# Attention with a second, transposed score product, and values and denominators of a group in one run of column-tiled products one step later

## The reference, cut to what matters

```
h = layernorm(x)
q = (h @ wq_w.T + wq_b).reshape(b, t, 32, 32)
k1 = h @ wk_w.T + wk_b            # one head of 32 for all
v1 = h @ wv_w.T + wv_b
scores = einsum('bqhd,bkd->bhqk', q, k1) / sqrt(32)
scores = where(causal, scores, -inf)
weights = softmax(scores)
attn = einsum('bhqk,bkd->bqhd', weights, v1)
x = x + attn.reshape(b, t, 1024) @ wo_w.T + wo_b
```

## Time and profile before

| | us |
|---|---|
| median of the runs | 3959.29 |
| profiled execution, span of the core | 3969.6 |
| TensorE matmul busy in it | 3404.7 |
| VectorE busy | 2089.3 |
| ScalarE busy | 1116.5 |
| GpSimd busy | 618.2 |

### The profile page before, as it was taken

The page is one execution under the profiler, slowest core; times in us unless marked ns, Lnnn a source line. Parts: engine busy times, 40 slices in busy tenths (PEclk is TensorE's granted clock), DMA queues, the critical chain, the costliest instruction groups (busy, mean ns, idle before and its releaser), DMA issues. The chain is left out here.

```text
span 3969.6 us, 53353 instructions
## 1 busy us (share of the span) xinstructions
PE 3404.7 (86%) x20224; PEld 2841.5 (72%) x20224; DVE 2089.3 (53%) x3582; ACT 1116.5 (28%) x2964; POOL 618.2 (16%) x754
## 2 busy tenths in 40 slices
PE   1898998998989989989999778878787878787868
PEld 1786887887868878878788356757575757666656
DVE  3463663654636626546466236555565646464633
ACT  2341442423414414324244013121212121121221
POOL 0001001000010010000100033223232323232311
PEclk9999999999999999999999778888898988888878
DMA  6322222222222222132221400000101010101000
GB/s 213 96 75 94 79 63 96 78 70 89 75 83 75 67 93 84 60 101 79 73 75 46 154 22 22 13 31 11 33 9 34 6 38 6 37 3 41 1 21 22
DMA packets 105455, 234.99 MB, mean 59 GB/s; under 512 B 20170, under 2 KB 38858, under 8 KB 105202
## 3 DMA queue, kind: packets, MB, share of 16 engines
q1 hardware_dynamic: 100544, 228.22, 18.6%
q10 hardware_dynamic: 4658, 3.22, 0.3%
HBM read 139.10 MB, written 41.94 MB: 46 GB/s over the span
## 5 line engine op out<-in xcount | busy, mean ns | idle before, releaser
L305 ACT ACTIVATE probs<-ps_attn,neg_max 128x128 f32<-128x128 f32 (+3 forms) x1024 | 534.8, 526 | 1070.5 <-DVE neg_max L398 1045.5
L557 PE MATMUL ps_attn<-probs_t,v_pad 128*128 128x128 f32 x5120 | 696.3, 277 | 17.5 <-DVE probs_t L408 15.9
L557 PEld LDWEIGHTS ps_attn<-probs_t,v_pad 128*128 128x128 f32 x5120 | 626.7, 192 | 33.6 <-DVE probs_t L408 28.2
L398 DVE TENSOR_REDUCE neg_max<-ps_attn 128x1 f32<-128x384 f32 (+3 forms) x704 | 449.8, 639 | 315.9 <-PE ps_attn L526 313.7
L408 DVE COPY probs_t<-ps_attn 128x512 f32<-128x512 f32 (+1 forms) x704 | 447.1, 636 | 272.4 <-PE ps_attn L544 272.4
L1182 PE MATMUL ps_mixer<-m_w_hi,m_xt_hi 128*128 128x512 f32 x1024 | 429.0, 419 | 77.1 <-DVE m_xt_lo L1021 77.1
L524 PE MATMUL ps_attn<-k_stack,q_stack 96*128 96x128 f32 (+3 forms) x1024 | 371.1, 398 | 72.9 <-issue 50.6
L1183 PE MATMUL ps_mixer<-m_w_hi,m_xt_lo 128*128 128x512 f32 x1024 | 415.6, 406 | 0.0
L1184 PE MATMUL ps_mixer<-m_w_lo,m_xt_hi 128*128 128x512 f32 x1024 | 414.2, 405 | 0.0
L544 PE MATMUL ps_attn<-ident_sb,probs 128*128 128x128 f32 x2560 | 397.5, 274 | 0.0
L544 PEld LDWEIGHTS ps_attn<-ident_sb,probs 128*128 128x128 f32 x2560 | 285.2, 142 | 20.3
(11 more groups left out here) (189 smaller groups left out, 5408.3 us busy)
## 6 DMA issues: line engine op xcount, KB each, us to landing
wq_hi<-wq_split SPq DMA_DIRECT2D x64, 512.0 KB, 3.6
wq_lo<-wq_split SPq DMA_DIRECT2D x64, 512.0 KB, 4.5
q_stack<-q_hi SPq DMA_DIRECT2D x512, 64.0 KB, 2.0
x_ring<-in_a_x SPq DMA_DIRECT2D x32, 512.0 KB, 4.1
q_stack<-q_lo SPq DMA_DIRECT2D x256, 64.0 KB, 2.0
r_ring<-in_a_x SPq DMA_DIRECT2D x32, 512.0 KB, 3.7
x<-r_ring SPq DMA_DIRECT2D x32, 512.0 KB, 2.6
m_xs<-x SPq DMA_DIRECT2D x32, 512.0 KB
```

The source lines that it names most:

```text
L305: exp = nc.scalar.activation(probs[:, s % P_RING, m * n:(m + 1) * n], ps[:, s % S_RING, m * n:(m + 1) * n], ACT.Exp, bias=neg_max[:, s % S ...
L398: nc.vector.tensor_reduce(neg_max[:, s % STAT, 0:len(heads)], ps[:, s % S_RING, 0:n * len(heads)].rearrange("p (j k) -> p j k", k=n), AX.X ...
L557: mm = nc.tensor.matmul(ps[:, 6 + g % 2, i * P:(i + 1) * P], v_pad[:, k, lead:lead + P], probs_t[:, u % T_RING, cols], start=(j == 0 and k ...
```

## The change

The attention function is rewritten; the mixer is not touched. What it does:

- Each score product is made twice. `scores` (queries on partitions) serve only for the row maxima (`tops`), for all 11 units of a group as before; the mask is now a float32r product, one per unit instead of one per head. The 16 maxima columns are transposed in one product (`tops_turned`), copied by ScalarE and written by one copy on SyncE's queue (`shift`) as a 97th row of `q_stack`, under which `k_stack` has a row of -1. `turned_scores` (keys on partitions, no mask, 11 units of at most 512 columns) then give score minus maximum already transposed.
- ScalarE takes the exponential of these straight into the tiles `pt` (no transposes, no copies); GpSimd sets what lies above the diagonal to zero (`cut`, four `affine_select` of 128x512 a group).
- One step later `weigh_all` multiplies values (`v_sb`, 128x32) and a tile of ones (128x32) with `pt` in float32: 4 key tiles x 2 x 4 heads = 32 products of 512 to 128 columns, each with 32 output partitions at 32*j. VectorE takes the reciprocal of the denominators (128x512) and multiplies (`divide`). This stands in place of the transposes, of the padded value products and of the `finish_` steps up to `finish_scale`; `finish_low` goes to GpSimd.
- There are no rows with barriers any more: steps M from -2 to 64 run through all 64 groups, written out, without a loop. Step M holds, in TensorE's order, the query projection of M+2, the maxima's transpose of M, scores 0 and 1 of M+1, the value products of M-1, then in turn the turned scores of M and the other scores of M+1. In a step with M+2 divisible by 8 the layer norm's transposes, the key and value projection and the whole query projection of the next row take the projection's place; a step with M divisible by 8 ends with the output projection of the row that is done.

The diff, cut to its core:

```diff
-    S_RING, P_RING, T_RING, STAT = 3, 3, 2, 8
-    T_LAG, AV_LAG = 2, 3
...
+    S_UNITS = [(3, (0,)), (3, (1,)), (3, (2,)), (3, (3,)), (2, (0,)), (2, (1,)), (2, (2,)), (2, (3,)), (1, (0, 1)), (1, (2, 3)),
+               (0, (0, 1, 2, 3))]
+    T_UNITS = [(0, (0,)), (0, (1,)), (0, (2,)), (0, (3,)), (1, (0,)), (1, (1,)), (1, (2,)), (1, (3,)), (2, (0, 1)), (2, (2, 3)),
+               (3, (0, 1, 2, 3))]
...
+                def stack(G):
+                    sp.wait_ge(qhi_done, G + 1)
+                    if G >= 2:
+                        sp.wait_ge(st_ready, U * (G - 1))
+                    for place, src in ((0, q_hi), (2, q_hi), (1, q_lo)):
+                        if place == 1:
+                            sp.wait_ge(qlo_done, G + 1)
...
+                def shift(G):
+                    sp.wait_ge(top_rows_done, G + 1)
+                    sp.dma_start(q_stack[KROWS:KROWS + 1, G % 2, :, :].bitcast(F32).rearrange("o j (i t) -> o (j i) t", t=P),
+                                 top_rows[:, :].bitcast(F32)).then_inc(top_in, DMA)
...
+                for M in STEPS:
+                    if inside(M):
+                        shift(M)
...
+                    if inside(M + 3):
+                        load_wq(M + 3)
...
+                    if inside(M + 2):
+                        stack(M + 2)
...
+                def cut(G, k):
+                    pool.wait_ge(exp_done, U * G + (4, 8, 10, 11)[k])
+                    diagonal = pt[k][:, :, 0:P]
+                    nc.gpsimd.affine_select(diagonal, diagonal, [[0, GH], [1, P]], ALU.is_ge, 0.0, base=0,
+                                            channel_multiplier=-1).then_inc(sel_done, 1)
...
+                def divide(G):
+                    dve.wait_ge(b_done, G + 1)
...
+                    nc.vector.reciprocal(att[:, :], ps[:, DEN, :]).then_inc(inv_done, 1)
+                    dve.wait_ge(inv_done, G + 1)
+                    nc.vector.tensor_tensor(att[:, :], ps[:, AV, :], att[:, :], ALU.mult).then_inc(att_done, 1)
...
+                    if inside(M + 1):
+                        tops(M + 1, (0, 1))
+                    if inside(M - 1):
+                        divide(M - 1)
+                    if inside(M + 1):
+                        tops(M + 1, (2, 3))
...
+                def scores(G, u):
+                    i, heads = S_UNITS[u]
+                    n, b = U * G + u, G // GROUPS
+                    width = (i + 1) * P
+                    if u == 0:
+                        pe.wait_ge(qs_in, (G + 1) * STACK)
...
+                    if n >= 2:
+                        pe.wait_ge(s_used, n - 1)
...
+                def turned_scores(G, u):
...
+                    if u == 0:
+                        pe.wait_ge(top_in, (G + 1) * DMA)
+                    if n >= 2:
+                        pe.wait_ge(exp_done, n - 1)
+                    for m, j in enumerate(heads):
+                        mm = nc.tensor.matmul(ps[:, ST0 + n % 2, m * width:(m + 1) * width], k_stack[:, b % 2, k * P:(k + 1) * P],
+                                              q_stack[:, G % 2, j, k * P:T], start=(m == 0), stop=(m == len(heads) - 1))
+                    mm.then_inc(st_ready, 1)
+
+                def weigh(G, blocks, last):
+                    for k in blocks:
+                        for bank, side in ((AV, v_sb[:, (G // GROUPS) % 2, k, :]), (DEN, ones[:, :])):
+                            for j in range(GH):
+                                mm = nc.tensor.matmul(ps[j * HEAD:(j + 1) * HEAD, bank, k * P:T], side, pt[k][:, j, :],
+                                                      start=(k == 0), stop=(k == TILES - 1))
+                    mm.then_inc(last, 1)
...
+                for M in STEPS:
+                    b = next_row(M)
+                    project = b is None and inside(M + 2)
+                    if project:
+                        q_part(M + 2, (0, 1, 2))
+                    if inside(M):
+                        tops_turned(M)
+                    if project:
+                        q_part(M + 2, (3,))
+                    if b is not None:
+                        transposes(b, 0)
+                    if inside(M + 1):
+                        scores(M + 1, 0)
+                        scores(M + 1, 1)
+                    if inside(M - 1):
+                        weigh_all(M - 1)
+                    for u in range(U):
+                        if inside(M):
+                            turned_scores(M, u)
+                        if u + 2 < U and inside(M + 1):
+                            scores(M + 1, u + 2)
+                        if u == 1 and b is not None:
+                            transposes(b, 1)
+                        if project and u in (1, 3, 4, 5):
+                            q_part(M + 2, ({1: 4, 3: 5, 4: 6, 5: 7}[u],))
+                        if u == 5 and b is not None:
+                            transposes(b, 2)
+                    if b is not None:
+                        transposes(b, 3)
+                        kv(b)
+                        q_part(M + 2, range(CH))
+                        values(b)
+                    if (b := last_row(M)) is not None:
+                        output(b)
```

More of the change, by code:

```diff
@@ L22, in attention_program @@
     KROWS = 3 * HEAD
[L24 to L27, removed]
-    S_RING, P_RING, T_RING, STAT = 3, 3, 2, 8
-    T_LAG, AV_LAG = 2, 3
[L30 to L39, removed]
+    NG = BATCH * GROUPS
+    S_UNITS = [(3, (0,)), (3, (1,)), (3, (2,)), (3, (3,)), (2, (0,)), (2, (1,)), (2, (2,)), (2, (3,)), (1, (0, 1)), (1, (2, 3)),
+               (0, (0, 1, 2, 3))]
+    T_UNITS = [(0, (0,)), (0, (1,)), (0, (2,)), (0, (3,)), (1, (0,)), (1, (1,)), (1, (2,)), (1, (3,)), (2, (0, 1)), (2, (2, 3)),
+               (3, (0, 1, 2, 3))]
+    U = len(S_UNITS)
+    S0, ST0, PROJ, AV, DEN, MISC = 0, 2, 4, 5, 6, 7
+    Y_TILES = 2 * TILES
+    DMA = 16
+    STACK = 3 * GH * DMA
     with ExitStack() as ctx:
@@ L55, in attention_program @@
         q_hi, q_lo = sb("q_hi", [P, T], F32R), sb("q_lo", [P, T], F32R)
[L56 to L64, removed]
+        q_stack = sb("q_stack", [KROWS + 1, 2, GH, T], F32R)
+        k_stack = sb("k_stack", [KROWS + 1, 2, T], F32R)
+        v_sb = sb("v_sb", [P, 2, TILES, HEAD])
+        ones = sb("ones", [P, HEAD])
+        pt = [sb(f"pt_{k}", [P, GH, T - k * P]) for k in range(TILES)]
+        top = sb("top", [P, P])
+        top_rows = sb("top_rows", [GH * TILES, P], F32R)
+        att = sb("att", [P, T])
         stats, mean_var = sb("stats", [P, 2, 2, 6]), sb("mean_var", [P, 2, 2])
@@ L85, in stage @@
         def stage(n):
-            s = r_ring[:, n % 2, :]
+            s = xr[:, n % 2, :]
             return s.rearrange("p (c m) -> p c m", c=CH) if n == 0 else s
@@ L595, in attention_program @@
-        row(None, 0)
-        with nc.Fori(0, BATCH - 1) as b:
-            row(b, b + 1)
-        row(BATCH - 1, None)
+        xr_in = [sem("xr_in_0"), sem("xr_in_1")]
+        stats_done, mv_done, eps_done, std_done, xn_done = (sem("stats_done"), sem("mv_done"), sem("eps_done"), sem("std_done"),
+                                                            sem("xn_done"))
+        xt_ready, xhi_done, xlo_done = sem("xt_ready"), sem("xhi_done"), sem("xlo_done")
+        kv_ready, kv_done, khi_done, k_done, vt_ready, v_done = (sem("kv_ready"), sem("kv_done"), sem("khi_done"), sem("k_done"),
+                                                                 sem("vt_ready"), sem("v_done"))
@@ new lines, in attention_program, with x_load, r_load, stored @@
+        r_bias, y_ready, y_added, x1_out = sem("r_bias"), sem("y_ready"), sem("y_added"), [sem("x1_out_0"), sem("x1_out_1")]
+        def x_load(b, t):
+            return (t if b == 0 else TILES * (2 * b - 1) + t) // 2 + 1
+        def r_load(b, t):
+            return (TILES * 2 * (b + 1) + t if b + 1 < BATCH else TILES * (2 * BATCH - 1) + t) // 2 + 1
+        def stored(b, t):
+            return 2 * b + t // 2 + 1
+        def next_row(M):
+            return (M + 2) // GROUPS if (M + 2) % GROUPS == 0 and M + 2 < NG else None
```

786 lines of the change are left out of this document (358 added, 428 removed).

## The result

The changed kernel takes 4260.05 us (median of 4 runs, 4256.55 to 4265.31) against 3961.93 us before (3958.81 to 3968.02): ratio 1.0746, 95% interval 1.0729 to 1.0763. It is 298 us slower; forecast were 478. The profiled execution has a span of 4254.8 us. The mixer's first operation stands at 2502.65 us instead of 2219.66, 283 later, and the span is 285 longer, so the loss lies in the attention.

The account below looks back on a forecast made before the run. TensorE's work alone was taken to bound the attention. Usual steps of 33.3 us make a row 324.2 against 267.4: 456 for eight rows plus 20 at the ends, so 3959 + 476 = 4435, said as 4440; range 4000 to 4760 (0.80).

Parts of the forecast that it names:

- Slower: Whole kernel: the changed kernel takes more time than the one before; chance 0.89.
- The gap: Before the scores: twelve q_stack copies land 9.3 us after the turned scores end; TensorE stands 6.3 us; nearly every step.
- The loop's wait: Turned and other scores in turn: 3.0 us reciprocal delays maxima, scores of unit 4 wait until 4.9; loop 12.4 us.
- The values: Value and denominator products of a group on TensorE: 8.9 us, being 8.5 plus 0.4 for start and end.
- two strips: Value products: two 32-wide column strips work at a time, 8.5 us; likeliest case, chance 0.53, own range 4240 to 4590.
- four strips: Rival, value products: all four column strips at once, 4.3 + 0.3 us a group; 4165 us in all, chance 0.20.
- The clock: Value products behind the wait for copies: 3 to 4 us at half speed, 2.0 us lost a step.
- The sum: Usual step: copies' wait 9.3, scores 0.7, value products 8.9, half-speed loss 2.0, loop 12.4; 33.3 against 23.95 us.
- No gap: Rival, before the scores: copies land before the scores ask, 430 us less, 4010 us in all; chance 0.07.
- one strip: Rival, value products: products one after the other, 17.4 us a group; 4985 us in all, chance 0.11.
- faster: Rival: TensorE's queue meets its waits, a step is its work, 21.1 us; 3620 us in all, chance 0.09.
- The point that decides: Waits and clock loss per step: below 5.7 us the change wins, above it loses; priced at 12.2.

Follow-up runs that it names:

- the copies on two queues: Changed kernel with six of the twelve q_stack copies per group issued by ScalarE instead of SyncE: 4047.2 us, ratio 1.0186 to the kernel before.
- the values before the scores: Changed kernel with the value products of M-1 ahead of scores 0 and 1 of M+1 on TensorE: 4103.6 us, ratio 1.0336 to the kernel before.
- the shorter filler: Changed kernel with 14 unused 512-column products put before the scores in most steps (another run had 24): 4184.6 us, ratio 1.0556 to the kernel before.
- Both edits together: Changed kernel with value products ahead of scores 0 and 1, and the division behind the maxima on VectorE: 3876.5 us, ratio 0.9768 to the kernel before.
- the earlier projection: Projection chunks 4 to 7 after loop units 0 to 3, added to values first, late division and copies on two queues: 3856.3 us, ratio 0.9707.
- One strip after another: Changed kernel with value and denominator products issued bank, head, key tile, so neighbours write the same 32 partitions: 4785.1 us, ratio 1.2053 to the kernel before.
- The late division alone: Changed kernel with the division of M-1 moved on VectorE behind the maxima of units 2 to 10: 4010.3 us, ratio 1.0107 to the kernel before.

## Why the prediction was right and wrong

**The sign and its causes: right.** Slower had 0.89, and both causes were named in their places. The gap is 9.2 us from the end of the turned scores to the scores in most steps, 9.4 in the mean (9.3 forecast). TensorE stands for 1.83 + 4.07 = 5.9 us in it in the step shown, 1.9 + 2.8 = 4.7 in the mean (6.3): the projection takes 4.6 us there, at half clock, where the forecast had it at full. The part of 1.9 has another releaser than forecast, the query weights, whose load I had not followed: it is issued when the last chunk is read and TensorE goes on with it 4.8 us later. Behind the copies all that cost nothing more; with the copies gone it is the next loss (the copies on two queues).

**The loop's wait: right.** The reciprocal took 3.36 us for 3.0, and S(4) started 4.89 us after the values (501.71 - 496.82), forecast 4.9. At full clock the loop takes 11.9 us, for the 12.4 followed.

**The values: wrong, 8.9 should be 4.4.** The failing step is "two strips at a time": I let a product overlap only with its next neighbour. At full clock the 32 products, 64 instructions, take 4.45 us (the values before the scores), which is the rival "four strips" (0.20) with its 4.3. Eight instructions of 256 columns start in two fours, 0.22 us apart: the two instructions of a product follow each other, and all four heads run side by side. The rule I had set as the rival holds here: the Trainium skill, TensorEngine Tiling (Array Packing), Theoretical Speedup, says up to four times for 32 outputs, and the trace agrees with 1.7 / 0.43. The draining at a switch of tiling mode, which its section Key Properties states, can be seen here as at most 0.15 us at the end of a run (4.45 less 4.3) and 0.08 before it (a mask starts 0.15 us before the values, 521.63 to 521.78, and 0.07 before a score product). Slack for it was fair, but the halving of the overlap had no row behind it.

**The clock: right behind the gap, wrong in the loop.** Forecast 2.0 us a step, behind the gap alone. There it is 2.3 in the mean of the 35 usual steps: 1.9 in the values (6.3 us instead of 4.4) and 0.4 in the two scores before them. The step that failed is that the loop was summed at full clock: its own wait of 2.5 us brings the clock down again, in the step shown for 6.3 us (501.71 to 508.00), and the loop takes 14.9 us there and 13.8 in the mean, not 12.4. A wait of 8.7 us was the only one that the earlier trace rows show, and I had not asked what one of 2.5 us does. The runs price both: at least 1.3 us a step behind the gap (the shorter filler), and about 2 behind the loop's wait (289 us for a reciprocal, of which its wait is 2.5 x 64 = 160). The third fall of the clock, behind the wait for the weights, the forecast did not have; the copies covered it.

**The sum.** From the end of one run of values to the end of the next the forecast was 12.4 + 9.3 + 0.7 + 8.9 + 2.0 = 33.3; measured in one step 14.9 + 9.2 + 7.0 = 31.1, in the mean of the 35 usual ones 13.8 + 9.4 + 7.6 = 30.8, and 30.5 in the six of the batch row shown. So in the mean +1.4 in the loop, +0.1 in the gap, -4.0 in scores and values: two errors of opposite sign. The steps at the row's change, cut the same way, were forecast at 54.4 and 70.0 and measured 50.9 and 66.3. Together (6 x 2.8 + 3.5 + 3.7) = 24 us a row or 192 for eight, which is the miss of 180. "TensorE busy under 7 tenths" was wrong too, it is 79%, as half clock stretches what counts as busy. The likeliest case, two strips, was the wrong one, and the time still lies inside the range that I gave it, 4240 to 4590. That is luck: with four strips and my clock I would have said 4165, 95 us too low, and what filled that in is the clock in the loop (1.4 us in most of the 64 steps).

**No gap, one strip, faster.** The versions that were run show each as the mechanism it was. Both edits together, with or without the two queues and the earlier projection, give 3856 to 3876, faster than before, though waits for weights and copies are left in them. One strip after another gives 4785, where 4985 was priced. The point that decides was given as 5.7 us a step of waits and clock; with values at 4.4 instead of 8.9 it moves to 10.2. The changed kernel is above it (30.5 - 16.6 = 13.9) and loses, both orders together are below it (4.7) and win. The late division alone, 25.2 - 16.6 = 8.6, should have won by it and is 1.1% slower: the point counts usual steps only, and the waits at a row's change come on top. That they make up the whole difference is argued and not shown.

## What to carry to other kernels

When an operation is made 32 times wider (a reciprocal of 16 columns to one of 512), look first at what stands behind it in its engine's order and whether TensorE's next buffer hangs on that; put it behind the last such operation, and put independent products where a wait is known. A wait of some 2.5 us in a tight stretch cost nearly double here (4.6 us in the mean, between 2.7 and 5.7), since in most steps the clock behind it was lost too. So look at all steps of a trace and not at one, and read TensorE's share of busy time together with its granted clock. Products with few output partitions gain the full factor by tiling only if neighbours in the order of issue lie in different strips: 13.0 us one strip after another, 4.45 in turn.

## What the hardware showed that was not expected

- A wait of 2.5 us in a loop that is otherwise full was enough for the granted clock to fall from 0.99 to 0.50 for the next 6.3 us, and one of 1.9 us before the projection for it to fall there. But it did not always: in 5 of 35 usual steps the clock stayed at 1.00 behind the 2.5 us.
- In the run strip by strip, a product with the ones starts at 571.41, before three instructions of value products that start at 571.62, 571.84 and 571.95, although all of the latter are issued before it. The same happens at each change of strip. Products of different strips don't keep the order of issue in their starts. The Trainium skill, TensorE: Matmul & The Clock Gate, under "What overlaps and what doesn't", states that they do in start and end; the trace of this run shows it otherwise for starts, and the measurement decides. Whether an end may be out of order as well can't be read from ends that are modelled, so a semaphore on the last product of such a run should be placed with care.
- From 16 to 512 columns the reciprocal costs 6.3 ns for each further column, (3357 - 243) / 496, more than the 5.5 between the two narrow ones.
